# Projections of an attention layer: a new plan of the PSUM banks, the rotated pair scaled in place, and units that lie together in DRAM

## The reference

```python
Q, K, V = (x @ W.T, split into 16 heads of 8, for W_Q, W_K, W_V)
Q, K    = q*cos + flip(q)*sin, k*cos + flip(k)*sin      # flip: (-second half, first half)
attn    = softmax(causal(Q K^T / sqrt(8)))
x       = layernorm(x + (attn V) @ W_O.T)
gates   = softmax(x @ Wg + bg); the two largest, rescaled to sum 1
x       = layernorm(x + sum over the two experts of gate * (gelu(x W1 + b1) W2 + b2))
```

## Time and profile before

| | |
|---|---|
| median of the runs | 833.98 us |
| the three runs | 836.16, 829.27, 833.98 us |
| profiled execution, its own time | 828.04 us |
| its span, first to last instruction | 825.9 us |
| outside the span | 2.1 us |
| PE, DVE, ACT, POOL busy in the span | 679.4, 591.8, 443.1, 326.4 us |
| granted TensorE clock, mean | 0.912 |
| DMA | 83.71 MB, mean 101 GB/s |

### The profile page before, as it was taken

The page is one execution under the profiler, slowest core; times in us unless marked ns, Lnnn a source line. Parts: engine busy times, 40 slices in busy tenths (PEclk is TensorE's granted clock), DMA queues, the critical chain, the costliest instruction groups (busy, mean ns, idle before and its releaser), DMA issues.

```text
span 825.9 us, 19171 instructions
## 1 busy us (share of the span) xinstructions
PE 679.4 (82%) x5560; PEld 362.0 (44%) x5561; DVE 591.8 (72%) x1467; ACT 443.1 (54%) x840; POOL 326.4 (40%) x577
## 2 busy tenths in 40 slices
PE   5858999999988899898889898897879956999830
PEld 2343333333433333334333343332269956989830
DVE  5957788888898988598988889798426721222266
ACT  1323566766546556455556664665736623656524
POOL 3863232243121256322227523134714464444551
PEclk9995699999989899798999999899979977999975
DMA  8767515100101102001011110100167744687924
GB/s 300 254 205 231 141 47 148 47 22 27 47 14 35 37 31 77 27 28 31 17 50 40 58 48 9 39 2 19 35 184 209 197 143 137 179 228 211 304 83 113
DMA packets 72169, 83.71 MB, mean 101 GB/s; under 512 B 9858, under 2 KB 53384, under 8 KB 71952
## 3 DMA queue, kind: packets, MB, share of 16 engines
q1 hardware_dynamic: 67728, 74.04, 30.8%
q0 software_dynamic: 4352, 8.53, 2.9%
HBM read 55.77 MB, written 26.90 MB: 100 GB/s over the span
## 4 chain that ended last, share of the span: by engine, by line
PE 43%; DVE 25%; issue 13%; SPq 8%; ACT 4%; another core or an unknown queue 2%; DMA 2%; POOL 2%; DVEq 0%; ACTq 0%; POOLq 0%
DVE mx L1128 13%; PE banks L722 13%; PE banks L678 9%; PE banks L704 5%; PE banks L780 3%; PE banks L791 3%; SPq L577 2%; PE banks L673 2%; SPq L571 2%; SPq L578 2%; ACT region L836 2%; PE banks L731 2%; DVE w_sb L915 1%; DVE w1e L909 1%
## 5 line engine op out<-in xcount | busy, mean ns | idle before, releaser
L1128 DVE TENSOR_REDUCE mx<-banks 128x1 f32<-128x512 f32 (+3 forms) x640 | 366.4, 631 | 51.4 <-PE banks L678 45.2
L836 ACT ACTIVATE region<-banks 128x1024 f32<-128x1024 f32 (+3 forms) x256 | 201.6, 841 | 164.0 <-PE banks L704 158.7
L678 PE MATMUL banks<-region 64*128 64x512 bf16 (+3 forms) x768 | 197.0, 351 | 18.1 <-DVE mx L1128 16.0
L704 PE MATMUL banks<-region 64*128 64x512 bf16 (+3 forms) x768 | 140.8, 342 | 12.1 <-ACT region L836 6.1
L722 PE MATMUL banks<-region 128*32 128x512 f32 (+3 forms) x1024 | 120.5, 544 | 0.9 <-POOL region L1379 0.8
L836 ACT ACTIVATE cs_sb<-banks 128x1024 f32<-128x1024 f32 (+2 forms) x128 | 91.3, 759 | 41.4 <-PE banks L704 40.6
L1389 POOL DMA_INDIRECT results<-region,dest x72 | 71.9, 999 | 102.5 <-DVE region L1256 74.6
L673 PE MATMUL banks<-mask_sb,half_sb 64*128 64x128 bf16 (+1 forms) x384 | 85.3, 253 | 29.2 <-DVE mx L1128 17.6
L1250 DVE TENSOR_TENSOR region<-banks,w1e 128x128 f32<-128x128 f32 x72 | 21.0, 291 | 109.6 <-PE banks L780 59.4
L1379 POOL TENSOR_SCALAR_AFFINE_SELECT region<-region 128x256 f32<-128x256 f32 x160 | 64.3, 410 | 85.2 <-ACT region L836 82.3
L791 PE MATMUL banks<-region,w1e 128*128 128x128 f32 x576 | 82.8, 290 | 18.4 <-ACT region L862 15.8
(11 more groups left out here) (177 smaller groups left out, 695.8 us busy)
## 6 DMA issues: line engine op xcount, KB each, us to landing
w1e<-in_w SPq DMA_DIRECT2D x72, 322.0 KB
region<-stack SPq DMA_DIRECT2D x128, 56.0 KB
region<-stack SPq DMA_DIRECT2D x64, 112.0 KB
stack<-x_sb SPq DMA_DIRECT2D x16, 384.0 KB, 3.3
region<-pairs SPq DMA_DIRECT2D x72, 66.0 KB
stack<-x_sb SPq DMA_DIRECT2D x16, 256.0 KB, 3.6
region<-results SPq DMA_DIRECT2D x8, 512.0 KB, 4.8
xT_sb<-in_xT SPq DMA_DIRECT2D x4, 512.0 KB, 12.2
```

The lines of the kernel that those rows point to most:

```text
L678: last = mm(ring[:, bank, m * n:(m + 1) * n], qst[rows, v % NG, sb_ // 4, slot_, sb_ % 4 * P:(sb_ % 4 + 1) * P], kst[rows, v % NG, slot_, ...
L704: last = mm(score[:, slot_, par, 0:n], kst[rows, u % NG, slot_, j * P:(j + 1) * P], qst[rows, u % NG, c, slot_, s0 - c * CH:s0 - c * CH + ...
L836: nc.scalar.activation(probs[i % 6][:, :, 0:n], score[:, i % 2, :, 0:n], ACT.Exp, scale=SCALE).then_inc(exp_done, 1)
L1128: read(v.tensor_reduce(dst, src, AX.X, ALU.max, negate=True))
```

## The change

- **Banks and PE's order.** The plain pair has banks 3 and 4, the flipped pair banks 5 and 6, for every chunk (one buffer instead of two). For chunk c PE makes the plain pair when DVE has read the last one (`plain_read`), the flipped pair when DVE has finished the last chunk's add (`rotated`), and then the values of chunk c-1 into bank 2 or 7. PE waits at first for the Q and K weights and the first 512 columns of x alone.
- **DVE.** The product with sin is written back to the flipped pair's banks in PSUM; the add reads `rot` from SBUF and the flipped pair from PSUM. The wait for POOL (`rem_done`) moves from ahead of the first product to ahead of the add.
- **ACT** copies the values chunk by chunk, each copy ahead of the next part-0 cast.
- **Layout.** The heads' feature rows are permuted (`order`) so that the 16 rows that one parity of a unit needs are adjacent; `stack` becomes `stack_q`, with the column half outside, and `stack_k`. `load_unit` is then six DMAs: four for Q with rows of 2 KB (112 KB each) and two for K with rows of 4 KB (224 KB each).
- **Order on SP.** The weights, columns and cos/sin come in pieces in the order of use; the constant fill is split into sequence 0, issued at the start, and sequences 1 to 3 (1.57 MB in two DMAs), issued behind `load_unit(0, 1)` and so ahead of the first `MROWS`. The load of x moves from unit 0's `MROWS` to unit 2's.

```diff
-        stack = nc.dram_tensor("stack", [2, B, ROWS // 8, H, 8, S], BF16, kind="Internal").ap()
+        stack_q = nc.dram_tensor("stack_q", [B, 2, ROWS // 8, P, CH], BF16, kind="Internal").ap()
+        stack_k = nc.dram_tensor("stack_k", [B, ROWS // 8, P, S], BF16, kind="Internal").ap()
...
+        PAIR = (RING, RING + 2)
+        V_BANK = (RING - 1, RING + 4)
...
-            sp.dma_start(w_sb[:, :, :], w).then_inc(weights_in, 16)
-            for b in range(B):
-                sp.dma_start(xT_sb[:, b * S:(b + 1) * S], xT[:, b * S:(b + 1) * S]).then_inc(xT_in[b], 16)
-                if b == 0:
-                    sp.dma_start(cs_sb[:, :, :], cs).then_inc(weights_in, 16)
...
+            sp.dma_start(w_sb[:, 0:4, :], w[:, 0:4, :]).then_inc(qk_weights_in, 16)
+            for i in range(2):
+                cols = slice(i * CH, (i + 1) * CH)
+                sp.dma_start(xT_sb[:, cols], xT[:, cols]).then_inc(xT_in[i], 16)
+                sp.dma_start(cs_sb[:, :, cols], cs[:, :, cols]).then_inc(cs_in[i], 16)
+            sp.dma_start(w_sb[:, 4:6, :], w[:, 4:6, :]).then_inc(vo_weights_in, 16)
...
             def load_unit(b, g):
...
+                for par in (0, 1):
+                    rows = slice(64 * par, 64 * par + ROWS)
+                    mine = slice(32 * g + 16 * par, 32 * g + 16 * par + 16)
+                    for c in range(2):
+                        sp.dma_start(qst[rows, g, c, :, :].rearrange("p s n -> p (s n)"),
+                                     stack_q[bass.ds(b, 1), c, :, mine, :].rearrange("o z (r s) n -> (o z) r (s n)", s=2)
+                                     ).then_inc(dma_unit[g], 16)
+                    sp.dma_start(kst[rows, g, :, :].rearrange("p s n -> p (s n)"),
+                                 stack_k[bass.ds(b, 1), :, mine, :].rearrange("o z (r s) n -> (o z) r (s n)", s=2)
+                                 ).then_inc(dma_unit[g], 16)
...
             load_unit(0, 1)
+            fill_rows(1, B - 1)
...
+            for c in range(NCH):
+                pe.wait_ge(xT_in[c if c < 2 else c // 2 + 1], 16)
+                if c >= 1:
+                    pe.wait_ge(plain_read, c)
+                project(c, 0).then_inc(plain_done, 1)
+                if c >= 1:
+                    pe.wait_ge(rotated, c)
+                project(c, 1).then_inc(flip_done, 1)
+                if c >= 1:
+                    values(c - 1)
+            values(NCH - 1)
 
             pe.wait_ge(masks_ready, 3)
-            pe.wait_ge(v_read, RING)
 
             def visit(e, r, at):
                 kind = e[0]
+                if r == V_BANK[0]:
+                    pe.wait_ge(v_read, NCH - 1)
...
             for c in range(NCH + 1):
+                if c >= 1:
+                    act.wait_ge(v_done, c)
+                    nc.scalar.copy(v_sb[:, 4 * (c - 1):4 * c, :],
+                                   banks[:, V_BANK[(c - 1) % 2], :].rearrange("p (t n) -> p t n", t=4)
+                                   ).then_inc(v_read, 1)
...
+                ve.wait_ge(plain_done, c + 1)
+                v.tensor_tensor(rot[:, i, 0, :, :], plain, cos, ALU.mult).then_inc(plain_read, 1)
+                ve.wait_ge(flip_done, c + 1)
+                v.tensor_tensor(flipped, flipped, sin, ALU.mult).then_inc(flip_scaled, 1)
                 if c >= 2:
                     ve.wait_ge(rem_done, c - 1)
-                v.tensor_tensor(rot[:, i, 0, :, :], banks[:, bank:bank + 2, :], cos, ALU.mult).then_inc(dve, 1)
-                link[0] += 1
-                v.tensor_tensor(rot[:, i, 1, :, :], banks[:, bank + 2:bank + 4, :], sin,
-                                ALU.mult).then_inc(proj_read, 1)
...
-                v.tensor_tensor(rem[:, i, 0, :, :], rot[:, i, 0, :, :], rot[:, i, 1, :, :],
-                                ALU.add).then_inc(rotated, 1)
+                ve.wait_ge(plain_read, c + 1)
+                ve.wait_ge(flip_scaled, c + 1)
+                v.tensor_tensor(rem[:, i, 0, :, :], rot[:, i, 0, :, :], flipped, ALU.add).then_inc(rotated, 1)
...
-                    elif v == 0:
+                    elif v == 2:
...
+    order = np.arange(D).reshape(NG, 2, 2, DK).transpose(0, 2, 3, 1).reshape(-1)
```

## The result

| | before | after |
|---|---|---|
| median | 834.39 us (827.58 to 838.60, 18 runs) | 824.54 us (818.47 to 832.82, 18 runs) |
| traced execution, its own time (span) | 828.04 us (825.9) | 823.58 us (821.8) |
| first QK | 87.0 us | 73.6 us |

By the medians the changed kernel is 9.9 us faster. The ratio is 0.9885, with a 95% interval of 0.9859 to 0.9911, which is 7.4 to 11.8 us. The median lies inside the forecast range, but the gain is 9.9 us where 15.5 were forecast. The traced execution of before was 6 us under its median, that of after only 1 us under, so the two spans say less than the two medians.

The account below looks back on a forecast made before the run. DVE was taken to bound the projections and pass A, with SP's loads causing the hole between. First QK 87.0 to 71.5 us, 15.5 earlier: 828.04 becomes 812.5, or 818.5 us against the median; 8-in-10 range 811 to 827.

Parts of the forecast that it names:

- the forecast's own bounds: Bounds on the total: gains of 17.7 + 1 and 13 - 3 us, so 815 to 824.
- a doubled sin: Rival in the projections: sin written to PSUM costs double, 2.42 us; 9 us gained, 825; chance 0.07.
- The start: Start of the projections: PE starts at 4.8 us, DVE's memset ends at 9.46, the first chunk's add at 14.0.
- The pace: Projections: one chunk every 4.65 us instead of 5.28, with add and sin each taken as 1.21.
- rival of a falling clock: Rival: the clock falls in the projections, 8.5 us a chunk, total 9 us slower, 843; chance 0.05.
- SP: SP's issue list: unit 0's loads 34.8 to 39.4 us, stores until 60.5, unit 1's loads 65.1, MROWS issued by 67.7.
- the third rival: Rival on SP: loads don't get cheaper, six at 1.55 us; 6 us gained, 828; chance 0.07.
- MROWS lands: Ahead of the first QK: unit 0's MROWS lands at 71.5 us, bounds 69 and 74.
- Pass A: Unit 0's pass A starts at 47.8 us and at DVE's pace allows QK 21.5 us later, at 69.3.
- the two conditions: The first QK is the later of pass A at 69.3 and MROWS at 71.5 us: 15.5 us earlier.
- past it the engines wait only for one another: Behind the first QK no row has a fixed time, so its whole shift moves everything behind it.
- The terms put at 0: Load of x at unit 2 (bounds -1 and +3), fewer loads of units 2 to 15, clock early in attention (up to 4.5 us).

Follow-up runs that it names:

- e2: The changed kernel with the two fills of sequences 1 to 3 issued behind unit 0's first MROWS instead of ahead of it; 819.14 us, ratio 0.982.
- e3: The changed kernel with sin's product written to SBUF again, so the add has both inputs in SBUF; 826.16 us, ratio 0.9892.
- e5: The changed kernel with the fills of sequences 1 to 3 behind MROWS and ACT copying chunk 6's values earlier; 820.76 us, ratio 0.9819.

## Why the prediction was right, and where it fell short

Direction and range held, and so did the mechanism up to the first QK. Two terms of the sum were too good; by the traces they come to some 6.2 us, where 5.6 are missing. That the median lies in the range owes something to luck: 824.5 is just outside the 815 to 824 that the forecast's own bounds gave, and the range reached 827 only for a doubled sin and the spread of the runs. The doubled sin did not happen; the stop, for which no price was set, filled its place.

- **The start.** PE at 4.28 (forecast 4.8), DVE's memset until 9.45 (9.46), chunk 0's add ends at 13.22 (14.0). The pair products overlapped the memset as argued.
- **The pace.** 4.66 us (4.65); add 1.22 and sin 1.23 (both taken as 1.21), L1350 2.13 (2.12). The rival of a doubled sin is out. So is the rival of a falling clock: PE is busy 22.66 of 23 us at a granted clock of 1.00. The Trainium skill's warning (TensorE: Matmul & The Clock Gate, A second HAM failure mode) that cycling through PSUM banks with short waits makes the clock swing, doesn't show here: the program has PE's flipped pair wait for DVE's add in every chunk, but the trace leaves PE next to no idle time in that stretch, and the clock at 1.00.
- **SP.** Six loads in 33.74 to 38.72 (34.8 to 39.4); loads of 112 and 224 KB cost 0.73 to 1.00 us, so the third rival is out too. The 28 stores ended at 60.09, after 21.3 us (60.5); unit 1's loads at 64.8 (65.1); MROWS issued by 67.84 (67.7).
- **MROWS lands, the first term that was mis-sized.** Forecast 71.5 with a store's 3.6 us and a little; it landed 6.6 us after its second issue, at 73.5, inside the bounds of 69 to 74. e2 shows that it was the fills: behind them 3.9 us of PE's wait, without them none.
- **Pass A.** Started at 46.56 and was held at its third item until 48.59 by the copy (47.8), and ended near 69.8 (69.3). The order of the two conditions was right: pass A first, MROWS last.
- **"past it the engines wait only for one another", the step that failed.** The sum carried the new time of the first QK to the end one for one, and the loads of units 2 to 15 were put at 0 because "SP waits there anyway". SP does wait there; but a load's price isn't only SP's time. Unit 9's, in their new form, meet unit 7 at a moment that brings a stop, and the unit is 5.2 to 6.5 us longer. Unit 11 gives 0.9 to 2.6 us back. The forecast had named a longer unit behind the first as what would make it wrong.
- **The terms put at 0 that held.** The load of x in unit 2: units 2 and 3 take 27.7 us in before and after. The clock: the first 7.7 us of attention still run at 0.50.
- **The sum again:** 15.5 forecast, less 2.1 for MROWS, less 5.85 - 1.7 for units 7 and 11: 9.2. Measured 9.9.
- **The bandwidth of the stores.** 7.24 MB in the 21.5 us from 38.7 on, 337 GB/s, against the 327 of the earlier trace rows. The Trainium skill's 358 (DMA: Bandwidth & Descriptors, Where 436 GB/s comes from) is passed in single slices of that view (up to 375) and not reached in the mean; the row was the better price here.

## What to carry to other kernels

When a transfer is moved or reshaped, look up everything that is issued beside it in every later stage, not only whether its queue has time to spare; here six loads instead of twelve, in another layout, came with a stop in a unit far behind. Where a stage at the front gets faster by less in the total than in its own stretch, compare the lengths of the later stages unit by unit in two traces of each kernel: scatter moves, a new stop stays at its place. DMAs that nothing needs soon (the fills here, 1.57 MB) belong behind the small one that the next stage waits for.

## What the hardware showed unexpectedly

- An operation of DVE whose inputs are one tile in PSUM and one in SBUF ran at 1.22 us for 128x1024 float32 beside POOL, with both inputs in SBUF at 2.91 and 2.88 (e3), and at 1.23 when POOL was idle (e3); POOL's own operation beside it took 2.13 and 3.12. Writing the result to PSUM in place cost the same 1.23.
- Nearly every load of 56 rows in the traces of before and after cost SP 0.73 to 1.02 us to issue, whether it moves 56, 112 or 224 KB.
- Two DMAs of 6 KB behind two of 768 KB landed 6.6 us after the second one's issue, though SP took only 1.8 us to issue the two; with the large ones behind them (e5) it was 3.9.
- Engines can hand over 5 to 6 us late, with nothing in their records to wait for, while loads and indirect DMAs are issued together (unit 7, in eight traces), and the same DMAs at the same place of the next pass (unit 11) bring no such stop; the granted clock falls to 0.50 for 7 to 10 us with it.
